# The low part of the shared expert's weights moves from VectorE, in one piece, to GpSimd, in three pieces

## The chip, the cores and the metric

The kernel runs on one core of one Trainium2 chip. The time is that of one execution on the device, in microseconds (us); three runs of the kernel before gave 1497.79, 1499.32 and 1503.46 us, median 1499.32 us. The program is written by hand for the core's engines: TensorE (PE) for matrix products, VectorE (DVE), ScalarE (ACT) and GpSimd (POOL) for elementwise work, SyncE (SP) for starting transfers. Each engine works through its own list in order; the lists meet only at semaphores.

## The reference, cut to what matters

One Perceiver layer over 1024 tokens of width 512: a cross attention, a self attention and a mixture of 16 experts with one shared expert, each behind a layer norm and added to its input.

```python
x = x + xattn(layernorm(x), ctx_512)
x = x + attn(layernorm(x))                 # ends with the product by w_o: 2048 -> 512
x = x + ffn(layernorm(x))

def ffn(x):
    w, sel = route(x)                      # sigmoid scores, best 2 of 4 groups, best 4 of 16 experts
    out = sum over experts e of w[e] * (silu(x @ g[e].T) * (x @ u[e].T)) @ d[e].T
    shared = (silu(x @ shared_gate.T) * (x @ shared_up.T)) @ shared_down.T
    return out + shared
```

## The kernel before, in words

Every matrix product is made of three passes over numbers split in two. A float32 operand a is split into a high part (a cast to the reduced format float32r) and a low part (a minus the high part); hi x hi, hi x lo and lo x hi are summed in PSUM (`mm3`, lines 71 to 73). So each operand costs one cast and one subtraction before TensorE can use it.

The change lies in the last stage, `build_moe`. Its first part handles the 1024 tokens in eight token tiles of 128 (NT = 8, counted from 0). I call it the projection. For token tile tt:

- TensorE makes the product by w_o, 16 blocks of three passes into one PSUM bank. Halfway through (after block 7) it transposes the normalised rows of the tile before, `turn(tt - 1)` (line 1936); after block 11 it makes the router's logits of the tile before; at the end come the sums that give tokens their places (`prefix(tt - 2)`).
- ScalarE casts the attention output to its high part in two halves (`ao_high`, line 1633), copies the high part of the transposed rows (line 1637) and makes the sigmoid (line 1641).
- GpSimd makes the low parts of the two halves (`ao_low`, line 1546, 128x1024 elements each), the reciprocal root of the layer norm (`root`, line 1551), and starts four indirect transfers that scatter rows to their experts' blocks (`scatter`, line 1556).
- VectorE adds the product to the residual (line 1723, named acc below), makes the mean and variance (lines 1726 to 1731), the places of tile tt - 2 (`slots`, lines 1788 to 1791), the normalised rows (`norm`, line 1738, `h_rows` in the trace), then the routing of tile tt - 1 (lines 1749 to 1784, with the low part of the transposed rows, line 1744, between its halves).

I call VectorE's and GpSimd's work for one value of tt a turn. GpSimd's turn is in this order: root(tt), ao_low, two scatters, ao_low, two scatters (the scatters only from tt = 2).

The shared expert's weights (128x3072 elements) are loaded into `raw[0]` (part of the tile `w_ahead`) at the start. In turn 1 ScalarE casts them (line 1659), which raises the semaphore sh_hi; VectorE makes their low part in one subtraction at the end of its turn 1 (line 1866), which raises sh_lo. TensorE waits for sh_lo after the projection, when it begins the shared expert. SP waits for it too, in its loop over tt = 2 to 7, after the load of tile 4: `raw[0]` can then take the weights of routed expert 1 (`w_exp[2]`), which GpSimd needs once the projection is over and all rows are scattered (line 1607).

Two places in the order of work matter. `turn(tt - 1)` needs `norm(tt - 1)`, and the product of tile tt cannot go on past its middle before it. And VectorE's acc of tile tt needs the end of tile tt's product.

Of the kernel before, what the change touches and what calls it, by code (L numbers as in the profile page):

```python
# [25 lines left out]
ALU = mybir.AluOpType  # L26
# [74 lines left out]
def f32(ap):  # L101

    return ap.bitcast(F32)
# [5 lines left out]
def wait(eng, sem, value):  # L109

    if not isinstance(value, int) or value > 0:
        eng.wait_ge(sem, value)
# [1235 lines left out]
NBLK = NE * NT + DUMMY  # L1348
XR, YR, HR = 4, 3, 3
SORT_AT = 8  # L1350
ON_WAY = 3

C_BIAS, C_TRI, C_TRIG, C_DIAG = 0, NE, NE + NE * NE, NE + NE * NE + NG * NG
# [20 lines left out]
def build_moe(nc, ctx, sem, t, keep):  # L1374
# [5 lines left out]
    wcol = gu + NIT * D  # L1380
# [6 lines left out]
    WS = keep["ws"]  # L1387
# [57 lines left out]
    raw = [ahead[:, j * wcol:(j + 1) * wcol] for j in range(2)]  # L1445
    shared = 3 * SLOT
# [25 lines left out]
    sh_hi, sh_lo, e0_hi, e0_lo = sem("sh_hi"), sem("sh_lo"), sem("e0_hi"), sem("e0_lo")  # L1472
# [19 lines left out]
    @block.sync  # L1492
    def _(sp):
        sp.dma_start(acc[:, 0:NT // 2, :], t["x1"][0:NT // 2].rearrange("t p c -> p t c")).then_inc(x1_in[0], 16)
        sp.dma_start(gate_f[:], t["gate_w"]).then_inc(gate_in, 16)
        sp.dma_start(con[:], t["route_c"].to_broadcast([P, C_END])).then_inc(con_in, 16)
        sp.dma_start(tri_p[:], t["tri_p"]).then_inc(con_in, 16)
        sp.dma_start(ones_p[:], t["ones_p"]).then_inc(con_in, 16)
        sp.dma_start(col_p[:], t["col_p"]).then_inc(con_in, 16)
        sp.dma_start(raw[0], t["w_exp"][0]).then_inc(raw_in[0], 16)  # L1500
        sp.dma_start(raw[1], t["w_exp"][1]).then_inc(raw_in[1], 16)
        sp.dma_start(acc[:, NT // 2:, :], t["x1"][NT // 2:].rearrange("t p c -> p t c")).then_inc(x1_in[1], 16)
        for tt in range(2, NT):
            sp.wait_ge(a_lo, 2 * tt - 2)
            sp.dma_start(A[tt % 2], t["ao"][tt]).then_inc(a_in[tt % 2], 16)
            if tt == 4:
                sp.wait_ge(sh_lo, 1)
                sp.dma_start(raw[0], t["w_exp"][2]).then_inc(raw_in[0], 16)
        sp.wait_ge(table_made, 2)
        for j in range(HR):  # L1510
            sp.wait_ge(scattered[j], 16 * TOPK * len(range(j, NT, HR)))

        def block_at(i):
            return sp.value_load(tab[0:1, 2 * NTILE + i:2 * NTILE + i + 1], min_val=0, max_val=NBLK - 1)

        def landed(i):
            sp.wait_ge(y_out[i % YR], 16 * (i // YR + 1))
            sp.sem_inc(y_landed, 1)

        def load_x(i):  # L1520
            wait(sp, x_turned, i - XR + 1)
            sp.dma_start(X[i % XR], t["xs"][bass.ds(block_at(i), 1)].rearrange("o p c -> p (o c)")).then_inc(
                x_in[i % XR], 16)

        for i in range(XR + 2):
            load_x(i)
        for i in range(NTILE):
            if i >= 1:
                landed(i - 1)
            sp.wait_ge(y_made, i + 1)  # L1530
            sp.dma_start(t["xs"][bass.ds(block_at(i), 1)].rearrange("o p c -> p (o c)"), Y[i % YR]).then_inc(
                y_out[i % YR], 16)
            if i + XR + 2 < NTILE:
                load_x(i + XR + 2)
        landed(NTILE - 1)
        for tt in range(NT):
            sp.wait_ge(comb, NT * (TOPK - 1) + tt + 1)
            sp.dma_start(t["out"][tt], acc[:, tt, :]).then_inc(out_sem, 16)
        sp.wait_ge(out_sem, 16 * NT)

    @block.gpsimd
    def _(pool):
        def ao_low(q):
            tt, hf = q // 2, q % 2
            pool.wait_ge(a_hi, q + 1)
            pool.tensor_tensor(AS[q][1], A[tt % 2][:, hf * hh:(hf + 1) * hh, :], f32(AS[q][0]),
                               ALU.subtract).then_inc(a_lo, 1)

        def root(tt):
            pool.wait_ge(ln3, 3 * tt + 3)  # L1550
            pool.tensor_tensor(rstd[tt % 2][:], var[tt % 2][:], eps_pow[:], ALU.pow).then_inc(rstd3, 1)

        def scatter(tt, k):
            if k == 0:
                pool.wait_ge(pos_made, tt + 1)
            pool.indirect_dma_start(rows, bass.IndirectOffsetOnAxis(ap=pos_i[:, tt, k:k + 1], axis=0),  # L1556
                                    HN[:, tt % HR, :], None).then_inc(scattered[tt % HR], 16)

        def slot(e):
            at = e % NSLOT * SLOT  # L1560
            return WS[:, at:at + wcol], WS[:, at + wcol:at + 2 * wcol]

        def expert_low(e):
            pool.tensor_tensor(slot(e)[1], raw[(e + 1) % 2], f32(slot(e)[0]), ALU.subtract).then_inc(w_ready, 1)  # L1564

        def expert_load(e):
            pool.wait_ge(w_ready, e - 1)
            pool.dma_start(raw[(e + 1) % 2], t["w_exp"][e + 1]).then_inc(pool_in[e % 2], 16)

        pool.sem_inc(a_lo, 1)  # L1570
        ao_low(1)
        ao_low(2)
        pool.wait_ge(fill_in, 16 * NBLK // NT)
        for tt in range(NT):
            root(tt)
            if 2 * tt + 3 < 2 * NT:
                ao_low(2 * tt + 3)
            if tt >= 2:
                scatter(tt - 2, 0)
                scatter(tt - 2, 1)  # L1580
            if 2 * tt + 4 < 2 * NT:
                ao_low(2 * tt + 4)
            if tt >= 2:
                scatter(tt - 2, 2)
                scatter(tt - 2, 3)
        for tt in range(NT - 2, NT):
            for k in range(TOPK):
                scatter(tt, k)
        pool.wait_ge(e0_lo, 1)
        pool.sem_inc(w_ready, 1)  # L1590
        expert_load(2)
        for e in range(1, NE):
            if e == NSLOT:
                pool.wait_ge(table_made, 2)
            if e == 1:
                pool.wait_ge(raw_in[0], 32)
            else:
                pool.wait_ge(pool_in[e % 2], 16 * (e // 2))
            if e == 1:
                pool.wait_ge(proj_half, 2 * NT)  # L1600
            elif e < NSLOT:
                pool.wait_ge(d_mm, NT)
            else:
                pool.wait_ge(tile_done, pool.value_load(cum_i[0:1, e - NSLOT:e - NSLOT + 1], min_val=1,
                                                        max_val=NTILE + 1))
            pool.sem_inc(slot_free, 1)
            pool.tensor_copy(slot(e)[0], raw[(e + 1) % 2]).then_inc(pool_hi, 1)  # L1607
            pool.wait_ge(pool_hi, e)
            expert_low(e)
            if e + 2 < NE:  # L1610
                expert_load(e + 2)
        pool.wait_ge(w_ready, NE)
        pool.wait_ge(sorted_made, 1)
        for g in range(NT * TOPK):
            k, tt = g // NT, g % NT
            if tt == 0:
                e = NE - TOPK + k
                pool.wait_ge(y_landed, pool.value_load(cum_i[0:1, e:e + 1], min_val=1, max_val=NTILE + 1))
                pool.sem_inc(gather_free, 1)
            if k < TOPK - 1 and g >= ON_WAY:  # L1620
                pool.wait_ge(g_in[(g - ON_WAY) % 5], 16 * ((g - ON_WAY) // 5 + 1))
            wait(pool, g_in[g % 5], 16 * (g // 5))
            pool.indirect_dma_start(G[g], None, rows,  # L1623
                                    bass.IndirectOffsetOnAxis(ap=pos_si[:, tt, k:k + 1], axis=0)).then_inc(
                                        g_in[g % 5], 16)
# [79 lines left out]
    def _(dve):  # L1705
# [146 lines left out]
        for tt in range(NT):  # L1852
            x2_stats(tt)
            if tt >= 2:
                slots(tt - 2)
            norm(tt)
            if tt == NT - 1:
                break
            if tt >= 1:
                route_groups(tt - 1)  # L1860
            h3_low(tt)
            if tt >= 1:
                route_experts(tt - 1)
            if tt == 1:
                dve.wait_ge(sh_hi, 1)
                dve.tensor_tensor(WS[:, shared + wcol:shared + 2 * wcol], raw[0], f32(WS[:, shared:shared + wcol]),
                                  ALU.subtract).then_inc(sh_lo, 1)
        last = NT - 1
        h3_low(last)
        route_groups(last - 1)  # L1870
# [44 lines left out]
        for i in range(NTILE + 1):  # L1915
# [4 lines left out]
            if i < NTILE:  # L1920
                gated(i)
            if SORT_AT <= i < SORT_AT + 9:
                sort_slots(i - SORT_AT)
            if i >= NTILE - 3:
# [6 lines left out]
    def _(pe):  # L1931
# [61 lines left out]
            if a == 1:  # L1993
                last.then_inc(a_mm, 1)

        pe.wait_ge(sh_lo, 1)
        shared_in(0, 0)
        turn(NT - 1)
        shared_in(0, 1)
# [25 lines left out]
        for tt in range(NT):  # L2025
# [3 lines left out]
            for k in range(NIT):  # L2029
                cols = turned_cols(tt)  # L2030
# [189 lines left out]
```

## Time and profile before

| what | value |
|---|---|
| runs | 1497.79, 1499.32, 1503.46 us |
| time of the profiled execution | 1495.92 us |
| its span in the trace | 1494.1 us |
| busy share of the span: PE, DVE, ACT, POOL | 90%, 54%, 49%, 39% |
| mean granted TensorE clock | 0.958 of full |
| projection (tiles 0 to 7), in the trace | about 1064 to 1178 us |

The span runs from the first to the last recorded instruction; the execution takes 1.8 us more. The busy shares are means over stages with different limits, so the projection is read by itself, from the timeline of each engine: start, duration, instruction, and in square brackets the idle time ahead of it with what ended it. A duration contains the time for which an instruction was held after its start.

### The profile page before, as it was taken

To read this page: it belongs to the slowest core of one execution; us is meant where nothing else is said; L and a number is where in the kernel's file an instruction comes from. 1 tells how busy PE (TensorE), PEld (TensorE's weight loads), DVE (VectorE), ACT (ScalarE), POOL (GpSimd) and SP (SyncE) were. 2 spreads that over 40 slices of the span, in tenths; PEclk is the share of its full clock that TensorE was granted. 3 is DMA by queue.
4 is the path that set the end of the run, shared out by engine and by line. 5 is a ranking of instruction groups with operands and counts; after the bars stand their busy time and mean duration, and the time that the engine had idled before them with its cause. 6 is when DMAs were issued, how large, how long until landed. Compare 5 with 4: busy or idle time off the path is not lost. (4 is left out here: it accounts for less than half of the span.)

```text
span 1494.1 us, 22797 instructions
## 1 busy us (share of the span) xinstructions
PE 1350.1 (90%) x7136; PEld 1107.6 (74%) x7136; DVE 800.1 (54%) x1372; ACT 730.0 (49%) x1736; POOL 585.9 (39%) x350
## 2 busy tenths in 40 slices
PE   5998699999999999999975999998789989999991
PEld 4776577878787878787854888887577867787771
DVE  4434466666666666666634444445278853433235
ACT  2443466565656565656524677777222213343330
POOL 2430233232323333232013333335446486427975
PEclk9998799999999999999987999999799999999996
DMA  5795413141414141412095211112543256536667
GB/s 215 242 285 173 161 66 132 67 159 58 167 53 172 50 175 49 175 49 106 9 323 181 89 64 50 50 50 92 208 149 121 82 184 228 171 124 225 227 210 226
DMA packets 78984, 209.79 MB, mean 140 GB/s; under 512 B 5888, under 2 KB 39168, under 8 KB 72960
## 3 DMA queue, kind: packets, MB, share of 16 engines
q1 hardware_dynamic: 69472, 163.78, 31.4%
q0 software_dynamic: 7136, 38.80, 7.7%
q10 hardware_dynamic: 2304, 6.29, 1.1%
q8 instruction: 40, 0.66, 0.2%
q14 instruction: 32, 0.26, 0.1%
HBM read 154.59 MB, written 92.01 MB: 165 GB/s over the span
## 5 line engine op out<-in xcount | busy, mean ns | idle before, releaser
L722 DVE TENSOR_TENSOR probsT_lo<-psTr,probsT_hi 128x512 fp32r<-128x512 f32 x256 | 176.7, 690 | 168.0 <-ACT probsT_hi L675 167.7
L675 ACT CAST probsT_hi<-psTr 128x512 fp32r<-128x512 f32 x256 | 150.1, 587 | 198.9 <-PE psTr L806 195.1
L806 PE MATMUL psTr<-ident,probs 128*128 128x128 f32 x1024 | 153.6, 274 | 11.3 <-DVE probsT_lo L722 5.2
L806 PEld LDWEIGHTS psTr<-ident,probs 128*128 128x128 f32 x1024 | 124.2, 141 | 50.4 <-DVE probsT_lo L722 13.5
L717 DVE TENSOR_REDUCE nmax<-psS 128x1 f32<-128x1024 f32 x128 | 155.5, 1215 | 9.3 <-PE psS L73 8.3
L588 POOL TENSOR_TENSOR w_slots<-ctx_f,w_slots 128x512 fp32r<-128x512 f32 x32 | 41.4, 1294 | 278.1 <-ACT w_slots L639 278.1
L632 ACT ACTIVATE probs<-psS,nmax 128x1024 f32<-128x1024 f32 x128 | 143.8, 1123 | 12.1 <-DVE nmax L717 12.1
L71 PE MATMUL psS<-w_slots 128*128 128x512 f32 x256 | 113.0, 441 | 3.7 <-DMA w_slots<-qe 2.8
L71 PE MATMUL psV<-probsT_hi,w_slots 128*128 128x512 f32 x256 | 114.7, 448 | 0.6
L71 PE MATMUL bank<-w_slots,ao_first_hi 128*128 (+1 forms) x244 | 102.8, 421 | 8.2 <-POOL w_slots L1564 4.5
L1564 POOL TENSOR_TENSOR w_slots<-w_ahead,w_slots 128x3072 fp32r<-128x3072 f32 x15 | 102.2, 6810 | 1.2
L73 PE MATMUL psS<-w_slots 128*128 128x512 f32 x256 | 101.9, 398 | 0.0
L72 PE MATMUL psS<-w_slots 128*128 128x512 f32 x256 | 101.3, 396 | 0.0
L73 PE MATMUL psV<-probsT_hi,w_slots 128*128 128x512 f32 x256 | 101.1, 395 | 0.0
L72 PE MATMUL psV<-probsT_lo,w_slots 128*128 128x512 f32 x256 | 100.2, 391 | 0.0
L71 PE MATMUL bank<-w_slots 128*128 128x512 f32 (+1 forms) x214 | 87.9, 411 | 8.8 <-DVE w_slots L1904 4.6
L73 PE MATMUL bank<-w_slots,ao_first_lo 128*128 (+1 forms) x244 | 95.8, 393 | 0.0
L72 PE MATMUL bank<-w_slots,ao_first_hi 128*128 (+1 forms) x244 | 95.1, 390 | 0.0
L1274 PEld LDWEIGHTS psSs<-kTs,qT 128*128 128x128 f32 x512 | 77.9, 196 | 9.7
L73 PE MATMUL bank<-w_slots 128*128 128x512 f32 (+1 forms) x214 | 84.9, 397 | 0.0
L72 PE MATMUL bank<-w_slots 128*128 128x512 f32 (+1 forms) x214 | 84.9, 397 | 0.0
L1904 DVE TENSOR_TENSOR w_slots<-bank,w_slots 128x256 fp32r<-128x256 f32 x47 | 19.9, 424 | 117.7 <-ACT w_slots L1686 117.6
(275 smaller groups left out, 3324.8 us busy)
## 6 DMA issues: line engine op xcount, KB each, us to landing
w_ahead<-w_exp POOLq DMA_DIRECT2D x14, 1536.0 KB, 7.8
qe<-stage SPq DMA_DIRECT2D x16, 1024.0 KB, 6.8
w_slots<-qe SPq DMA_DIRECT2D x16, 1024.0 KB, 4.9
wraw<-w_pairs SPq DMA_DIRECT2D x8, 1792.0 KB, 11.2
early<-xs SPq DMA_DIRECT2D x47, 256.0 KB, 3.0
xs<-h_rows SPq DMA_DIRECT2D x47, 256.0 KB, 2.5
early<-ctx SPq DMA_DIRECT2D x16, 512.0 KB, 11.6
ao<-attn_out SPq DMA_DIRECT2D x32, 256.0 KB, 2.4
```

Of the source, the lines that this page charges most:

```text
L71: pe.matmul(out, lhs[0], rhs[0], start=start, stop=False, skip_group_check=True)
L72: pe.matmul(out, lhs[0], rhs[1], start=False, stop=False, skip_group_check=True)
L73: return pe.matmul(out, lhs[1], rhs[0], start=False, stop=stop, skip_group_check=True)
L588: pool.tensor_tensor(CT.lo[:, cols[0], cols[1]], CX[:].rearrange("p (h s) -> p h s", s=S), f32(CT.hi[:, cols[0], cols[1]]), ALU.subtract). ...
L632: act.activation(PR[np_][:, rt, :], psS[rt % 2][:], ACT.Exp, bias=nmax[np_][:, rt:rt + 1], accum_out=rsum[np_][:, rt:rt + 1]).then_inc(exp ...
L675: act.copy(PT[k % PTN].hi[:], psT[slot][:]).then_inc(turned_hi, 1)
L717: dve.tensor_reduce(nmax[np_][:, rt:rt + 1], psS[rt % 2][:], AX.X, ALU.max, negate=True).then_inc(max_made, 1)
L722: dve.tensor_tensor(out, psT[slot][:], f32(hi), ALU.subtract).then_inc(turned_free, 1)
L806: last = pe.transpose(psT[slot][:, q * P:(q + 1) * P], src(q), ident[:])
L1274: last = pe.matmul(psS[j][:, h, :], QB[j][:, h].rearrange("p b s -> p (b s)"), KB[kt][:, g, :], start=False, stop=h == REP - 1, skip_group ...
L1564: pool.tensor_tensor(slot(e)[1], raw[(e + 1) % 2], f32(slot(e)[0]), ALU.subtract).then_inc(w_ready, 1)
L1904: dve.tensor_tensor(HT[i % 2][1], psHT[i % 2][:, 0:I].rearrange("p (k x) -> p k x", k=NIT), f32(HT[i % 2][0]), ALU.subtract).then_inc(ht_l ...
```

## The change

VectorE's subtraction at the end of its turn 1 is taken out. GpSimd makes the same low part in three subtractions of 128x1024 elements, one at the end of its turns 1, 2 and 3 (behind the scatters, where there are any). Each waits for sh_hi and raises sh_lo by one, so TensorE and SP wait for 3 instead of 1. SP's wait, with the load of `w_exp[2]` behind it, moves from behind the load of tile 4 to behind that of tile 6.

```diff
+SHARED_AT = (1, 2, 3)
...
-            if tt == 4:
-                sp.wait_ge(sh_lo, 1)
+            if tt == 6:
+                sp.wait_ge(sh_lo, len(SHARED_AT))
                 sp.dma_start(raw[0], t["w_exp"][2]).then_inc(raw_in[0], 16)
...
+        def shared_low(part):
+            n = wcol // len(SHARED_AT)
+            cols = slice(part * n, (part + 1) * n)
+            pool.wait_ge(sh_hi, 1)
+            pool.tensor_tensor(WS[:, shared + wcol:shared + 2 * wcol][:, cols], raw[0][:, cols],
+                               f32(WS[:, shared:shared + wcol][:, cols]), ALU.subtract).then_inc(sh_lo, 1)
...
             if tt >= 2:
                 scatter(tt - 2, 2)
                 scatter(tt - 2, 3)
+            if tt in SHARED_AT:
+                shared_low(SHARED_AT.index(tt))
...
-            if tt == 1:
-                dve.wait_ge(sh_hi, 1)
-                dve.tensor_tensor(WS[:, shared + wcol:shared + 2 * wcol], raw[0], f32(WS[:, shared:shared + wcol]),
-                                  ALU.subtract).then_inc(sh_lo, 1)
...
-        pe.wait_ge(sh_lo, 1)
+        pe.wait_ge(sh_lo, len(SHARED_AT))
```

VectorE's list from the end of its turn 1 to the start of turn 2, before (`choice_x` to `choice_weight` are the routing of tile 0, `acc` is the residual sum of tile 2):

```order
L1779 TENSOR_TENSOR choice_x<-choice,scores 128x64
L1780 TENSOR_REDUCE choice_w<-choice_x 128x4
L1781 TENSOR_REDUCE choice_sum<-choice_w 128x1
L1782 TENSOR_SCALAR choice_sum<-choice_sum 128x1
L1783 RECIPROCAL choice_sum<-choice_sum 128x1
L1784 TENSOR_SCALAR choice_weight<-choice_w,choice_sum 128x4
L1866 TENSOR_TENSOR w_slots<-w_ahead,w_slots 128x3072
L1723 TENSOR_TENSOR acc<-bank,acc 128x512
```

and the same place in the changed kernel, whose lines are numbered ten higher:

```order
L1792 TENSOR_SCALAR choice_sum<-choice_sum 128x1
L1793 RECIPROCAL choice_sum<-choice_sum 128x1
L1794 TENSOR_SCALAR choice_weight<-choice_w,choice_sum 128x4
L1733 TENSOR_TENSOR acc<-bank,acc 128x512
L1736 BN_STATS st_0<-acc 128x6
```

The residual sum of tile 2 now stands directly behind the routing of tile 0.

GpSimd's list from the end of its turn 1 to the start of its turn 4, in the changed kernel (L1568 is a piece, `rstd` is root, L1547 is ao_low, L1557 the scatters, two to a row):

```order
L1547 TENSOR_TENSOR ao_first_lo<-early,ao_first_hi 128x1024
L1568 TENSOR_TENSOR w_slots<-w_ahead,w_slots 128x1024
L1552 TENSOR_TENSOR rstd_0<-var_0,eps_pow 128x1
L1547 TENSOR_TENSOR w_slots<-early,w_slots 128x1024
L1557 DMA xs<-h_rows,slot_int 18432x512 x2
L1547 TENSOR_TENSOR ao_first_lo<-early,ao_first_hi 128x1024
L1557 DMA xs<-h_rows,slot_int 18432x512 x2
L1568 TENSOR_TENSOR w_slots<-w_ahead,w_slots 128x1024
L1552 TENSOR_TENSOR rstd_1<-var_1,eps_pow 128x1
L1547 TENSOR_TENSOR w_slots<-early,w_slots 128x1024
```

Before, root of the next tile stands where the pieces stand; the first piece comes directly behind an ao_low, the second (and the third, a turn later) behind two scatters.

## Rows read from the trace of the kernel before

**Rows 1.** The page: span and instructions.
```profile
span 1494.1 us, 22797 instructions
```
**Rows 2.** Timeline, TensorE: turn of tiles 2 and 4 (tile tt's transposes).
```profile
1112.17 1.11 PE L1936 MATMUL bank<-ident,h_rows 128*128 128x128 f32 x4 [3.83 <-DVE h_rows L1738]
1142.17 0.66 PE L1936 MATMUL bank<-ident,h_rows 128*128 128x128 f32 x4 [0.64 <-DVE h_rows L1738]
```
**Rows 3.** Busy time by stretch: PE, PEld, DVE, ACT, POOL, clock, DMA share, GB/s.
```profile
1102.50:1113.00 10.50, 6.67 (x32) 5.38 (x31) 9.75 (x18) 1.05 (x1) 3.88 (x3) 0.92 0.45 158
1113.00:1118.00 5.00, 5.00 (x14) 3.94 (x13) 4.79 (x10) 1.53 (x2) 4.11 (x4) 0.50 0.82 268
```
**Rows 4.** Timeline, ScalarE: casts released by the ends of tiles 2, 3, 4.
```profile
1102.53 1.05 ACT L1633 CAST w_slots<-early 128x1024 fp32r<-128x1024 f32 x1 [2.72 <-PE bank L73]
...
1122.51 1.05 ACT L1633 CAST w_slots<-early 128x1024 fp32r<-128x1024 f32 x1 [2.72 <-PE bank L73]
...
1135.73 1.05 ACT L1633 CAST w_slots<-early 128x1024 fp32r<-128x1024 f32 x1 [2.72 <-PE bank L73]
```
**Rows 5.** Timeline, VectorE: ends of turns 1 to 3, starts of turns 2 to 5.
```profile
1103.11 0.23 DVE L1784 TENSOR_SCALAR choice_weight<-choice_w,choice_sum 128x4 f32<-128x4 f32 x1
1103.37 3.36 DVE L1866 TENSOR_TENSOR w_slots<-w_ahead,w_slots 128x3072 fp32r<-128x3072 f32 x1
1106.65 0.68 DVE L1723 TENSOR_TENSOR acc<-bank,acc 128x512 f32<-128x512 f32 x1
...
1120.54 0.23 DVE L1784 TENSOR_SCALAR choice_weight<-choice_w,choice_sum 128x4 f32<-128x4 f32 x1
1122.51 0.69 DVE L1723 TENSOR_TENSOR acc<-bank,acc 128x512 f32<-128x512 f32 x1 [1.74 <-PE bank L73]
...
1136.29 0.23 DVE L1784 TENSOR_SCALAR choice_weight<-choice_w,choice_sum 128x4 f32<-128x4 f32 x1
1136.56 0.69 DVE L1723 TENSOR_TENSOR acc<-bank,acc 128x512 f32<-128x512 f32 x1
...
1150.60 0.69 DVE L1723 TENSOR_TENSOR acc<-bank,acc 128x512 f32<-128x512 f32 x1
```
**Rows 6.** Timeline, GpSimd: last instructions of turns 1 to 3, root(4), first expert cast.
```profile
1097.26 2.37 POOL L1546 TENSOR_TENSOR ao_first_lo<-early,ao_first_hi 128x1024 fp32r<-128x1024 f32 x1 [2.64 <-ACT ao_first_hi L1633]
...
1118.84 0.96 POOL L1556 DMA_INDIRECT xs<-h_rows,slot_int  x1 [0.31 <-issue]
...
1134.26 0.96 POOL L1556 DMA_INDIRECT xs<-h_rows,slot_int  x1 [0.31 <-issue]
1138.71 0.57 POOL L1551 TENSOR_TENSOR rstd<-var,eps_pow 128x1 f32<-128x1 f32 x1 [3.48 <-DVE var L1731]
...
1211.12 2.78 POOL L1607 CAST w_slots<-w_ahead 128x3072 fp32r<-128x3072 f32 x1
```
**Rows 7.** Three lines of VectorE: duration ns min/median/max, first and last start.
```profile
L1769 DVE TENSOR_TENSOR cmp_experts<-masked x8: 412/1368/2374, 1097.5 to 1191.9; 128x256 f32<-128x256 f32 x8
L1770 DVE TENSOR_TENSOR cmp_experts<-masked x8: 410/416/2593, 1099.8 to 1192.2; 128x256 f32<-128x256 f32 x8
L1791 DVE CAST slot_int<-slot_all x8: 170/2368/2417, 1109.3 to 1198.5; 128x4 int32<-128x4 f32 x8
```
**Rows 8.** Timeline near 645 us: GpSimd, and VectorE beside it.
```profile
644.99 2.14 POOL L127 TENSOR_TENSOR kv_rope_second<-early 128x1024 f32<-128x1024 f32 x1
...
645.88 0.17 DVE L772 RECIPROCAL rinv<-rsum 128x4 f32<-128x4 f32 x1
```
**Rows 9.** TensorE after two idle times elsewhere, and the stretch after the first.
```profile
141.03 0.46 PE L71 MATMUL psE<-w_slots 64*128 64x512 f32 x1 [2.24 <-DVE stage L348]
1302.93 0.49 PE L71 MATMUL bank<-w_slots 128*128 x1 [2.15 <-DVE w_slots L1904]
142.00:146.00 4.00, 4.00 (x9) 2.19 (x8) 1.97 (x3) 1.76 (x3) 0.00 (x0) 0.50 0.12 33
```
**Rows 10.** The page's list of transfers: an expert's weights, us to landing.
```profile
w_ahead<-w_exp POOLq DMA_DIRECT2D x14, 1536.0 KB, 7.8
```

## The prediction

> **What bounds the kernel now.** I read the page first: the span is 1494.1 us [rows 1], and the profiled execution took 1495.92 us, 1.8 more. That is 3.40 us under the median of the runs, 1499.32. I sum against the profiled execution and add these 3.40 us at the end. Then I went to the chain of waits of the projection, which passes through VectorE's acc and norm and comes back to TensorE at its transposes. So I read the timelines of TensorE, VectorE and GpSimd side by side.
>
> Two things are to be seen. First, TensorE stands still for 3.83 us in the middle of tile 3, at the transposes of tile 2, because `h_rows` is late [rows 2]. Its granted clock is 0.92 over the stretch with the stop and 0.50 in the 5 us behind it, the lower of its two levels, 1.2 GHz [rows 3]. ScalarE's casts show what this costs: tile 3 takes 1122.51 - 1102.53 = 19.98 us, tile 4 takes 1135.73 - 1122.51 = 13.22 us [rows 4]. The difference is 6.76 us: 3.83 of standing still and 2.93 of slow clock.
>
> The cause is the instruction that the change removes: VectorE's L1866 starts at 1103.37 and the next acc only at 1106.65 [rows 5], while tile 2's product was ready at 1102.53.
>
> Second, VectorE is the bound by itself in the turns behind. From acc at 1136.56 to acc at 1150.60 it takes 14.04 us [rows 5] against TensorE's 13.22, and TensorE waits 0.64 us at the transposes of tile 4 [rows 2]. It does so again, with the same time, for tiles 5 and 6. So what VectorE loses in turn 3 is not made up before the projection's end, and what it wins counts only as far as it wins it. Tile 7 and all that follows hang on this chain and move as one.
>
> VectorE is slow there because it is held. L1770 normally takes 416 ns and once 2593, L1769 412 and up to 2374, the cast L1791 170 and up to 2417 [rows 7]; each long one begins while GpSimd is in an ao_low of 2.37 us [rows 6] and ends with it. Not every instruction is held: a reciprocal, with one SBUF input, took 0.17 us at 645.88, in the middle of GpSimd's 2.14 us [rows 8]. Held are those with two SBUF inputs (L1769, L1770), a cast and the `h_rows` TENSOR_SCALAR from SBUF to SBUF.
>
> **Part 1: the subtraction leaves VectorE, piece 1 comes to turn 1.** Removed: 1106.65 - 1103.37 = 3.28 us between the routing and acc [rows 5]. Piece 1 has the shape of an ao_low, 128x1024, so 2.37 us [rows 6]. ScalarE's cast has raised sh_hi long before, so it begins at once behind the ao_low that ends at 1097.26 + 2.37 = 1099.63, and lasts to 1102.0. VectorE is then in the middle of L1769 to L1771, all with two SBUF inputs. One of them is held: 2593 - 416 = 2177 ns, 2.18 us [rows 7]. Bounds: 1.96 by L1769, 2.25 by L1791 [rows 7], and nothing if VectorE gets in first each time. I take 2.18 because L1770's row is the one where it lost against GpSimd with its neighbour just finished. Acc of tile 2 comes 3.28 - 2.18 = 1.10 us earlier.
>
> The stop at the transposes of tile 2 shrinks to 3.83 - 1.10 = 2.73 us. If the clock falls again, tile 3 ends at 1122.51 - 1.10 = 1121.41. If it holds, the product would be 2.93 us earlier still, but then VectorE is the later one (part 2).
>
> **Part 2: piece 2 in turn 2.** GpSimd's last scatter ends at 1118.84 + 0.96 = 1119.80 [rows 6], now 1118.70, so the piece ends at 1121.07, or up to 0.3 later, the gap that GpSimd leaves ahead of a scatter [rows 6]. L1784 would start at 1120.54 - 1.10 = 1119.44 [rows 5] and, as a TENSOR_SCALAR from SBUF to SBUF, is held until then. Acc of tile 3 can start at 1121.1 to 1121.4. Tile 3's product ends at 1121.41. Cost 0: VectorE's old wait of 1.74 us for TensorE [rows 5] is the cover. It is used up, though, so a clock that holds brings at most some 0.3 us.
>
> **Part 3: piece 3 in turn 3.** The last scatter ends at 1134.26 + 0.96 = 1135.22 [rows 6], the piece at 1137.59 in the old times. L1784 stood at 1136.29 and acc at 1136.56 [rows 5]; now acc cannot start before 1137.6 to 1137.9. That costs 1.05 to 1.35 us, and here there is no cover: VectorE was 0.83 us behind TensorE already (1136.56 against 1135.73, [rows 4, 5]). I take 1.2. Below: 0, if a TENSOR_SCALAR of four elements is not held. Above: 1.8, if L1782, 0.4 us ahead of it, is held too.
>
> The Trainium skill (SBUF — State Buffer, "Who interferes with whom") says that the port pair shared by VectorE and GpSimd is an exclusive lock, so whoever starts first blocks the other for the whole instruction, and that a VectorE instruction with two SBUF inputs is hit by a GpSimd one that reads SBUF. The long L1769 and L1770 agree. By this rule moving work to GpSimd pays only where VectorE has no such instruction meanwhile, and each of the three pieces falls on one.
>
> The same skill (VectorE: DVE Perf Modes, "Mode 2×_2P") gives tensor_scalar between SBUF tiles the mode that takes both ports when the outermost dimension above one is even, which holds for the four columns of L1784 and not for the one of L1782. By it part 3 costs about 1.2; without it, 0. No row shows L1784 beside a long GpSimd instruction.
>
> **What else moves.** GpSimd's roots stand behind the pieces. The tightest is root(4), which begins at 1138.71 after 3.48 us of idle time [rows 6]; piece 3 is done 0.8 to 1.1 us earlier, and root(4) itself moves back with VectorE. Nothing waits. SP's load of expert 1's weights goes from 1107 to about 1138 us; it lands in about 7.8 us [rows 10] and is used at 1211.12 [rows 6]. Behind it on SP stands only the load of tile 7, released at about 1142. TensorE's wait for sh_lo comes 40 us after piece 3. All these cost 0; the cover of the load is some 65 us.
>
> **The sum.** -3.28 + 2.18 + 0 + 1.2 = +0.1 us. The profiled execution would take 1496.0 us, the median 1499.32 + 0.1 = 1499.4. The gain of turn 2 is handed back in turn 3.
>
> **Rivals.**
>
> (a) The clock falls in tile 5 (slower). With part 3 the stop at the transposes of tile 4 grows from 0.64 to 1.84 us [rows 2]. For it: after an idle time of 2.24 us the granted clock was 0.50 soon behind [rows 9]. Against: after 2.15 us matmuls went on at full pace [rows 9]. [...] Price: 2.93 less the 0.83 us by which VectorE is behind, 2.1. Time 1499.4 + 2.1 = 1501.5; with part 3 at 1.8, 1502.1.
>
> (b) L1784 isn't held, so pieces 2 and 3 cost nothing. Then -1.10 stands: 1498.2. If the clock also holds after 2.73 us, acc of tile 3 follows VectorE: 1120.77 - 1.10 = 1119.67, which is 2.84 earlier than 1122.51: 1496.5. For it: pieces 2 and 3 lie mostly beside short one-input instructions. Against: L1791, also four columns, is held [rows 7].
>
> (c) The pieces hold VectorE nowhere, the full gain. Acc of tile 2 at 1103.37, one turn of 14.04 later acc of tile 3 at 1117.41 instead of 1122.51: -5.1, 1494.2. Even here VectorE's pitch eats part of the 6.76. Against it stand the long rows [rows 7].
>
> (d) The change doesn't do what it says, because GpSimd's pieces come late and push its root, and with it norm: only if a piece took over 3.3 us. No row of that shape does.
>
> **Chances.** Forecast 0.60 (own range 1498.9 to 1500.3), (a) 0.14, (b) 0.16, (c) 0.08, (d) 0.02. A difference of 0.5%, 7.5 us, is about what a measurement of this kernel can tell from no change, and no case reaches it: the largest, (c), is 0.34%. What is left is scatter of the runs, whose three times lie within 5.7 us. So faster 0.04, same 0.92, slower 0.04. The range goes from just inside (c) to just above (a): 1495.2 to 1502.6.
>
> **What would show it.** Right: no L1866; three GpSimd subtractions of 2.4 us ending near 1102, 1121 and 1137.7; a long duration of L1769, L1770 or L1771 near 1102 and of L1784 (four columns) in turns 2 and 3; acc of tile 2 at about 1105.5; the stop at the transposes of tile 2 at 2.7 us, and of tile 4 at 1.8. Wrong: L1784 at 0.23 us beside a piece (b), acc of tile 2 at 1103.4 (c), or a granted clock of 0.5 in tile 5 (a).

## The result, and the profile after

The changed kernel is slower: median 1504.47 us (22 runs, 1501.36 to 1507.68) against 1500.80 us (22 runs, 1497.79 to 1507.90) for the kernel before, run beside it. The ratio is 1.0022, 95% interval 1.0013 to 1.0032, that is 3.3 us slower (2.0 to 4.8). The forecast was +0.1 us.

The page of the changed kernel gives the span of its profiled execution:

```profile
span 1501.8 us, 22798 instructions
```

That is 7.7 us over the span of before [rows 1], more than the runs differ. The acc of VectorE divides it: 1.67 us lie ahead of acc of tile 1 (1091.23 against 1089.56), where the programs are alike; 3.86 between acc of tile 1 and of tile 7; 2.17 behind. The change acts in the middle stretch, and 3.86 us agrees with the 3.3 of the runs. Of the 2.17 behind, 1.25 lie between acc of tile 7 and the next sum into acc, behind the projection, where TensorE stands still for 2.51 us in both kernels and its clock falls behind that stop in the changed kernel alone (the last section comes back to this). Executions of one kernel differ by several us elsewhere, so from here on I read distances within the projection and not spans.

VectorE's timeline in the changed kernel, the acc of tiles 1 to 7 (start, duration, instruction, idle time ahead with its cause). It answers to [rows 5]:

```profile
1091.23 0.69 DVE L1733 TENSOR_TENSOR acc<-bank,acc 128x512 f32<-128x512 f32 x1 [5.53 <-PE bank L73]
...
1107.24 0.69 DVE L1733 TENSOR_TENSOR acc<-bank,acc 128x512 f32<-128x512 f32 x1
...
1124.14 0.69 DVE L1733 TENSOR_TENSOR acc<-bank,acc 128x512 f32<-128x512 f32 x1
...
1141.37 0.69 DVE L1733 TENSOR_TENSOR acc<-bank,acc 128x512 f32<-128x512 f32 x1
...
1156.11 0.69 DVE L1733 TENSOR_TENSOR acc<-bank,acc 128x512 f32<-128x512 f32 x1 [0.50 <-PE bank L73]
...
1170.16 0.69 DVE L1733 TENSOR_TENSOR acc<-bank,acc 128x512 f32<-128x512 f32 x1
...
1183.38 0.69 DVE L1733 TENSOR_TENSOR acc<-bank,acc 128x512 f32<-128x512 f32 x1 [1.11 <-PE bank L73]
```

From one acc to the next I call the length of a turn. Before: 17.09, 15.86, 14.05, 14.04, 14.04, 13.21 for turns 1 to 6, 88.29 in all. After: 16.01, 16.90, 17.23, 14.74, 14.05, 13.22, 92.15 in all. Turn 1 won 1.08 us, turn 2 lost 1.04, turn 3 lost 3.18, turn 4 lost 0.70.

VectorE's timeline shows why: here are the instructions that were held, and `choice_weight` beside them, which was not (its line is 1794 here, 1784 before; L1784 here is the selection `sel`):

```profile
1099.20 2.37 DVE L1779 TENSOR_TENSOR cmp_experts<-masked 128x256 f32<-128x256 f32 x1
...
1101.50 2.62 DVE L1780 TENSOR_TENSOR cmp_experts<-masked 128x256 f32<-128x256 f32 x1
...
1119.41 3.00 DVE L1784 TENSOR_SCALAR sel<-rank 128x16 f32<-128x16 f32 x1
...
1123.88 0.23 DVE L1794 TENSOR_SCALAR choice_weight<-choice_w,choice_sum 128x4 f32<-128x4 f32 x1
...
1136.84 3.14 DVE L1787 TENSOR_TENSOR choice<-rank,route_rows 128x64 f32<-128x64 f32 x1
```

and GpSimd's timeline round the pieces (L1568), which answers to [rows 6]:

```profile
1098.92 2.37 POOL L1547 TENSOR_TENSOR ao_first_lo<-early,ao_first_hi 128x1024 fp32r<-128x1024 f32 x1 [2.64 <-ACT ao_first_hi L1643]
1101.25 2.59 POOL L1568 TENSOR_TENSOR w_slots<-w_ahead,w_slots 128x1024 fp32r<-128x1024 f32 x1
...
1119.02 0.96 POOL L1557 DMA_INDIRECT xs<-h_rows,slot_int  x1 [0.30 <-issue]
1120.01 2.36 POOL L1568 TENSOR_TENSOR w_slots<-w_ahead,w_slots 128x1024 fp32r<-128x1024 f32 x1
...
1136.48 0.96 POOL L1557 DMA_INDIRECT xs<-h_rows,slot_int  x1 [0.31 <-issue]
1137.47 2.42 POOL L1568 TENSOR_TENSOR w_slots<-w_ahead,w_slots 128x1024 fp32r<-128x1024 f32 x1
```

Three things are to be seen. In turn 1, ao_low and piece 1 stand back to back, and each holds one instruction, L1779 and then L1780, until its own end. In turns 2 and 3 the held instruction is not `choice_weight`, as forecast, but `sel` and `choice`, eight and six instructions ahead of it. And it starts 0.60 and 0.63 us before the piece's recorded start, while the last scatter still runs, yet ends with the piece (1122.41 against 1122.37; 1139.98 against 1139.89).

TensorE's timeline shows who waits for that (L1958 is the sum over the selection for the token places, L1942 the transposes; to be read beside [rows 2]), and lines of busy time by stretch show the clock behind the last two stops (PE, PEld, DVE, ACT, POOL, granted clock, DMA share, GB/s; beside [rows 3]):

```profile
1105.77 0.40 PE L1958 MATMUL bank<-sel,tri_tokens 128*128 128x16 f32 x2 [1.66 <-DVE sel_before L1786]
...
1112.83 0.66 PE L1942 MATMUL bank<-ident,h_rows 128*128 128x128 f32 x4 [0.86 <-DVE h_rows L1748]
...
1122.67 0.40 PE L1958 MATMUL bank<-sel,tri_tokens 128*128 128x16 f32 x2 [2.34 <-DVE sel_before L1786]
...
1146.93 1.11 PE L1942 MATMUL bank<-ident,h_rows 128*128 128x128 f32 x4 [3.25 <-DVE h_rows L1748]
```

```profile
1123.00:1126.00 3.00, 3.00 (x10) 2.43 (x10) 2.48 (x9) 0.00 (x0) 0.00 (x0) 0.51 0.00 0
1146.00:1153.00 7.00, 6.07 (x28) 5.24 (x28) 6.63 (x16) 1.53 (x2) 5.58 (x5) 0.76 0.70 224
```

The stop of 3.83 us in tile 3 is gone, divided into 1.66 at the end of tile 2 and 0.86 at the transposes, without a fall of the clock. In its place stand 2.34 us at the end of tile 3 and 3.25 us at the transposes of tile 4. The clock falls behind both: the mean granted clock is 0.51 from 1123 to 1126 us, practically the lower level, and 0.76 over the seven us round the second stop, because the first matmuls run at the lower level.

### The profile page after: what moved, and what is told of

Same layout as the page of the kernel before. It is cut to its first block and busy times, and to the rows that moved or that the text cites. A ratio compares the mean times of both kernels' runs of the same rounds, so it can differ in the third digit from the quotient of the medians.

```text
span 1501.8 us, 22798 instructions
## 1 busy us (share of the span) xinstructions
PE 1357.7 (90%) x7136; PEld 1111.9 (74%) x7136; DVE 805.6 (54%) x1371; ACT 730.3 (49%) x1736; POOL 593.7 (40%) x353
## 5 line engine op out<-in xcount | busy, mean ns | idle before, releaser
L632 ACT ACTIVATE probs<-psS,nmax 128x1024 f32<-128x1024 f32 x128 | 143.7, 1123 | 12.2 <-DVE nmax L717 12.2
L71 PE MATMUL bank<-w_slots 128*128 128x512 f32 (+1 forms) x214 | 89.1, 416 | 8.5 <-DVE w_slots L1910 4.4
L73 PE MATMUL bank<-w_slots 128*128 128x512 f32 (+1 forms) x214 | 86.0, 402 | 0.0
L72 PE MATMUL bank<-w_slots 128*128 128x512 f32 (+1 forms) x214 | 85.9, 401 | 0.0
```

What stands on the lines that cost most here:

```text
L71: pe.matmul(out, lhs[0], rhs[0], start=start, stop=False, skip_group_check=True)
L72: pe.matmul(out, lhs[0], rhs[1], start=False, stop=False, skip_group_check=True)
L73: return pe.matmul(out, lhs[1], rhs[0], start=False, stop=stop, skip_group_check=True)
L632: act.activation(PR[np_][:, rt, :], psS[rt % 2][:], ACT.Exp, bias=nmax[np_][:, rt:rt + 1], accum_out=rsum[np_][:, rt:rt + 1]).then_inc(exp ...
```

## The experiments

The table gives the length of VectorE's turns in each kernel's profiled execution, in us; kernels 2, 3, 7 and 8 were run once, for this profile. The lengths repeat within 0.05 us where nothing acts on them, so differences of a few tenths can be read from one profile.

| kernel | turn 1 | 2 | 3 | 4 | 5 | 6 | sum | ratio of times to before (95%) |
|---|---|---|---|---|---|---|---|---|
| before | 17.09 | 15.86 | 14.05 | 14.04 | 14.04 | 13.21 | 88.29 | |
| changed | 16.01 | 16.90 | 17.23 | 14.74 | 14.05 | 13.22 | 92.15 | 1.0022 (1.0013 to 1.0032) |
| 1: low part left out | 14.04 | 14.05 | 14.04 | 14.03 | 14.04 | 13.21 | 83.41 | 0.9991 (0.9963 to 1.0019) |
| 2: piece 3 only | 13.82 | 14.07 | 16.86 | 14.02 | 14.05 | 13.18 | 86.00 | |
| 3: piece 2 only | 13.82 | 16.88 | 14.02 | 14.03 | 14.03 | 13.22 | 86.00 | |
| 4: pieces ahead of scatters | 16.02 | 16.25 | 16.24 | 14.40 | 14.04 | 13.22 | 90.17 | 1.0014 (0.9990 to 1.0038) |
| 5: pieces beside acc | 14.01 | 14.29 | 14.23 | 14.02 | 14.05 | 13.21 | 83.81 | 0.9972 (0.9958 to 0.9986) |
| 6: on VectorE in turn 0 | 14.07 | 14.06 | 14.04 | 14.05 | 14.04 | 13.21 | 83.47 | 0.9970 (0.9954 to 0.9987) |
| 7: before, load moved | 17.09 | 15.91 | 14.05 | 14.04 | 14.03 | 13.22 | 88.34 | |
| 8: pieces behind the selection | 16.03 | 16.82 | 16.56 | 14.01 | 14.03 | 13.22 | 90.67 | |

**Experiment 1: what the removed instruction is worth.** Edit, on the kernel before; the low part of the shared expert's weights is left out by it:

```diff
-                dve.tensor_tensor(WS[:, shared + wcol:shared + 2 * wcol], raw[0], ...).then_inc(sh_lo, 1)
+                dve.sem_inc(sh_lo, 1)
```

> The kernel before with VectorE's subtraction left out and nothing in its place (the low part of the shared expert's weights isn't made; the rest is unchanged). What the removed instruction is worth by itself. Theory A (VectorE's pitch is the bound behind it): acc of tile 2 comes 3.3 us earlier, turn 2 takes VectorE's own 14.0 us, acc(1) to acc(7) is 88.3 - 5.1 = 83.2 us, ratio to before 0.9966. Rival (TensorE's stop and slow clock were the whole cost): 6.8 us less, 81.5 us, ratio 0.9955.

Measured: 83.41 us from acc of tile 1 to that of tile 7, 4.88 less than before, where theory A said 5.1 and the rival 6.8. VectorE's timeline, acc of tiles 1 to 3 and 7:

```profile
1088.90 0.69 DVE L1723 TENSOR_TENSOR acc<-bank,acc 128x512 f32<-128x512 f32 x1 [5.54 <-PE bank L73]
...
1102.94 0.69 DVE L1723 TENSOR_TENSOR acc<-bank,acc 128x512 f32<-128x512 f32 x1 [0.26 <-DVE choice_weight L1784]
...
1116.99 0.69 DVE L1723 TENSOR_TENSOR acc<-bank,acc 128x512 f32<-128x512 f32 x1
...
1172.31 0.69 DVE L1723 TENSOR_TENSOR acc<-bank,acc 128x512 f32<-128x512 f32 x1 [1.11 <-PE bank L73]
```

Acc of tile 3 doesn't wait for TensorE: VectorE's own 14.04 us is the length of each turn. The 0.26 us ahead of acc of tile 2 go with the semaphore that VectorE still raises there; without it turn 1 is 13.82 (experiments 2 and 3). So taking the whole instruction off VectorE is worth 4.9 us here, 5.1 without the semaphore, and not TensorE's stop and slow clock of 6.76. The interval of the timed runs, 0.9963 to 1.0019, leaves out the rival's 0.9955 and has theory A's 0.9966 at its edge, but it can't tell this kernel from the one before.

**Experiments 2 and 3: one piece at a time.** Edit, on the changed kernel (with the waits for sh_lo set to 1): piece 3 only, and likewise piece 2 only (`part != 1`); the other two thirds of the low part are left out:

```diff
         def shared_low(part):
+            if part != 2:
+                return
```

> The changed kernel with only the piece of turn 3 made (the other two thirds of the low part are left out). Theory H (each GpSimd piece holds VectorE): turn 2 takes 14.0 us instead of 16.9, turn 3 stays at 17.2 (a hold of about 2.9 us), tile 5 still has its stop and slow clock, so turn 4 is 14.7. Rival L (turns 2 and 3 are long because of the moved load or of work that GpSimd has piled up): turn 3 falls back to about 14.0 as well.

> The changed kernel with only the piece of turn 2 made (the other two thirds are left out). Theory H: acc(1) to acc(2) is 13.8 us, turn 2 is 14.0 + 2.9 = 16.9, turns 3 and 4 are 14.0 each, no slow clock in tile 5. Rival L: turn 2 at 14.0 or turn 3 still long.

Measured: the piece alone makes its turn long, 16.86 in turn 3 and 16.88 in turn 2, and no other turn. In both kernels SP's load stands at its new place, so rival L falls. VectorE's timeline in the kernel with piece 3 only, and then in the one with piece 2 only:

```profile
1134.37 3.01 DVE L1786 TENSOR_SCALAR sel<-rank 128x16 f32<-128x16 f32 x1
```

```profile
1117.94 3.00 DVE L1786 TENSOR_SCALAR sel<-rank 128x16 f32<-128x16 f32 x1
```

The selection is held for 3.0 us in either; 3.01 - 0.17 = 2.84 is what the turn gained over 14.04 (2.82). Expectations of experiment 2 that missed: turn 3 is 16.86 us and not 17.2, and turn 4 is 14.02 and not 14.7, because the slow clock in tile 5 did not come with piece 3 alone. TensorE's timeline there:

```profile
1137.64 0.40 PE L1960 MATMUL bank<-sel,tri_tokens 128*128 128x16 f32 x2 [2.27 <-DVE sel_before L1788]
...
1144.73 0.66 PE L1944 MATMUL bank<-ident,h_rows 128*128 128x128 f32 x4 [0.91 <-DVE h_rows L1750]
```

The hold is paid at the end of tile 4's product (2.27 us), which leaves 0.91 for the transposes. In turn 3 of the changed kernel it was `choice` that was held, behind the selection. TensorE got past the tile's end and the whole delay came at the transposes, 3.25 us. So which of two neighbours is held decides where TensorE stands still.

It does not decide by itself whether the clock falls. In turn 2 the changed kernel and experiment 3 hold the same instruction and stop TensorE at the same place, for 2.34 and 2.33 us. In the changed kernel the clock then falls to 0.51 (the line from 1123 to 1126 above); in experiment 3 it stays at full:

```profile
1121.50:1124.50 3.00, 3.00 (x16) 2.52 (x16) 2.48 (x9) 0.00 (x0) 0.00 (x0) 1.00 0.00 0
```

No run here shows why. What it costs is shown: with the clock at full, turn 3 of experiment 3 takes 14.02 us.

**Experiment 4: pieces ahead of the last two scatters.** Edit, on the changed kernel:

```diff
+            if tt in SHARED_AT:
+                shared_low(SHARED_AT.index(tt))
             if tt >= 2:
                 scatter(tt - 2, 2)
                 scatter(tt - 2, 3)
-            if tt in SHARED_AT:
-                shared_low(SHARED_AT.index(tt))
```

> The changed kernel with the pieces of turns 2 and 3 ahead of the last two scatters instead of behind them, so directly behind an ao_low. Theory S (a piece queued behind a scatter takes hold of VectorE about 0.6 us before its recorded start, so that place costs 2.9 and not 2.2): turn 2 is 14.0 + 2.2 = 16.2 us instead of 16.9, turn 3 16.2 instead of 17.2, acc(1) to acc(7) 1.7 to 2.4 us shorter than the changed kernel's 92.1, ratio to before 1.001. Rival (a piece costs the same wherever it stands): within 0.3 us of 92.1, ratio 1.0025.

Measured: turns 2 and 3 are 16.25 and 16.24 us, as theory S said (16.2), and the sum is 1.98 shorter than the changed kernel's. Turn 2 on VectorE and then on GpSimd:

```profile
1117.31 2.44 DVE L1779 TENSOR_TENSOR cmp_experts<-masked 128x256 f32<-128x256 f32 x1
1119.68 2.61 DVE L1780 TENSOR_TENSOR cmp_experts<-masked 128x256 f32<-128x256 f32 x1
```

```profile
1117.08 2.38 POOL L1547 TENSOR_TENSOR ao_first_lo<-early,ao_first_hi 128x1024 fp32r<-128x1024 f32 x1
1119.40 2.61 POOL L1568 TENSOR_TENSOR w_slots<-w_ahead,w_slots 128x1024 fp32r<-128x1024 f32 x1
```

The same work costs 2.20 us here (16.25 - 14.05) and 2.8 behind a scatter. It still costs almost the whole piece. The timed ratio, 0.9990 to 1.0038, can't tell this kernel from the changed one, nor from the one before.

**Experiment 5: pieces beside VectorE's unshared work.** Edit, on the changed kernel:

```diff
             pool.wait_ge(sh_hi, 1)
+            pool.wait_ge(routed, part + 1)
...
                 route_experts(tt - 1)
+            if tt in SHARED_AT:
+                dve.sem_inc(routed, 1)
```

> The changed kernel in which each piece also waits for the end of VectorE's routing of its turn (a semaphore that VectorE raises just ahead of acc), so that it runs beside acc, the statistics and the variance, which have at most one SBUF input and no two-port form. Theory H: those aren't held; the piece of 2.4 us outlasts them by about 0.3 to 0.4 and delays root by as much. acc(1) to acc(2) 13.8 us, turns 2 to 4 about 14.4 each, acc(1) to acc(7) 84.0 to 84.8 us (before 88.3, changed 92.1), ratio to before 0.997. No long duration in the routing beyond that of ao_low. Rival (GpSimd holds VectorE's statistics and residual sum too): each turn 16 us or more, 90 us, ratio 1.001.

Measured: 83.81 us, ratio 0.9972 (0.9958 to 0.9986), faster than both kernels. VectorE from acc of tile 3 on, then GpSimd:

```profile
1119.96 0.69 DVE L1734 TENSOR_TENSOR acc<-bank,acc 128x512 f32<-128x512 f32 x1 [0.23 <-DVE choice_weight L1795]
1120.81 0.69 DVE L1737 BATCH_NORM_STATS2 st<-acc 128x6 f32<-128x512 f32 x1 [0.16 <-DVE acc L1734]
...
1122.14 0.28 DVE L1800 TENSOR_TENSOR choice_x<-choice,slot_of 128x64 f32<-128x64 f32 x1
...
1122.91 2.61 DVE L1749 TENSOR_SCALAR h_rows<-acc,mv,rstd 128x512 f32<-128x512 f32 x1
```

```profile
1119.94 2.40 POOL L1569 TENSOR_TENSOR w_slots<-w_ahead,w_slots 128x1024 fp32r<-128x1024 f32 x1 [1.51 <-DVEq L1876]
1122.30 0.57 POOL L1552 TENSOR_TENSOR rstd<-var,eps_pow 128x1 f32<-128x1 f32 x1
```

Beside the piece (1119.94 to 1122.34) acc and the statistics take their 0.69 us. Only L1800, with two SBUF inputs, is touched, for 0.05 us at the piece's end. Root follows the piece at once, about 0.2 us later than the variance would allow, but that costs nothing: turn 4 has a late root too and takes 14.02. What turns 1 to 3 lose (14.01 against 13.82, 14.29 and 14.23 against 14.05) is the semaphore that VectorE raises ahead of acc, about 0.2 us each; turn 4 has none. The rival falls. The same three subtractions on the same engine cost 8.3 us less, 83.81 against 92.15, for one semaphore.

**Experiment 6: the work stays on VectorE, in turn 0.** Edit, on the kernel before:

```diff
-            if tt == 1:
+            if tt == 0:
                 act.wait_ge(raw_in[0], 16)
...
-            if tt == 1:
+            if tt == 0:
                 dve.wait_ge(sh_hi, 1)
```

> The kernel before (VectorE makes the low part in one piece) with ScalarE's cast and VectorE's subtraction moved from turn 1 to turn 0, where VectorE waits 5.5 us for TensorE. Theory P (VectorE's pitch is what counts, and only from turn 1 on): acc(0) to acc(1) longer by 0 to 0.5 us because ao_low and the subtraction hold each other, acc(1) to acc(2) 13.8 to 14.1, then 14.0 each: acc(0) to acc(7) 96.4 to 97.0 us against 101.3 before and 105.2 changed, ratio to before 0.9968. Rival (the subtraction, held by or holding ao_low, only shifts TensorE's stop to tile 2): acc(0) to acc(7) stays within 1 us of 101.3.

Measured: acc of tile 0 to acc of tile 7 is 96.47 us (13.00 + 83.47), within the expected 96.4 to 97.0; ratio 0.9970 (0.9954 to 0.9987). VectorE, then GpSimd:

```profile
1093.59 3.35 DVE L1866 TENSOR_TENSOR w_slots<-w_ahead,w_slots 128x3072 fp32r<-128x3072 f32 x1
...
1099.20 0.69 DVE L1723 TENSOR_TENSOR acc<-bank,acc 128x512 f32<-128x512 f32 x1 [2.27 <-PE bank L73]
```

```profile
1093.97 5.21 POOL L1546 TENSOR_TENSOR ao_first_lo<-early,ao_first_hi 128x1024 fp32r<-128x1024 f32 x1 [2.65 <-ACT ao_first_hi L1633]
```

The hold works the other way round too: VectorE's subtraction began first and ran its normal 3.35 us, and ao_low, begun 0.38 later, took 5.21 us instead of 2.38. TensorE waited 0.17 us for it. VectorE still waits 2.27 us for TensorE ahead of acc of tile 1, so the subtraction is free.

**Experiment 7: the moved load alone.** Edit, on the kernel before: `if tt == 4:` to `if tt == 6:` in SP's loop.

> The kernel before with only SP's load of expert 1's weights moved from behind the load of tile 4 to behind that of tile 6. All theories of mine: no cost, acc(1) to acc(7) 88.3 us, and the first cast of expert weights on GpSimd follows the last scatter as before. Rival L (the moved load delays something): any pitch of turns 4 to 7 over 14.1 us or GpSimd waiting for the weights.

Measured: 88.34 us against 88.29, and GpSimd's first cast of expert weights begins at 1212.93, behind the last scatter (1211.38 + 0.96) and the start of a transfer, with no wait for the weights. No cost, rival L falls a second time.

**Experiment 8: pieces behind the selection.** Edit, on the changed kernel:

```diff
             pool.wait_ge(sh_hi, 1)
+            pool.wait_ge(sel_made, SHARED_AT[part])
```

> The changed kernel in which each piece also waits for VectorE's selection of its turn (the sum sel_before, which raises a semaphore just ahead of choice). In the changed kernel the selection itself was held from 0.6 us before the piece's recorded start. Theory W (GpSimd reaches for the shared port as soon as the piece's semaphores are up, even while the scatter ahead of it is still recorded): the selection passes at 0.17 us, one of the two or three instructions with two SBUF inputs right behind it is held until the piece ends, turns 1 to 3 lose 2.2 to 2.6 us each, 16.3 to 16.6 us in turns 2 and 3, TensorE doesn't wait for the selection at the ends of tiles 2 to 4 any more, acc(1) to acc(7) about 90 to 91 us. Rival D (the scatter's descriptor writing itself holds VectorE there): the selection or the add is still held while the scatter runs, turns 2 and 3 stay at 16.9 and 17.2 us.

Measured: turns 2 and 3 on VectorE, then on GpSimd:

```profile
1119.53 0.17 DVE L1785 TENSOR_SCALAR sel<-rank 128x16 f32<-128x16 f32 x1
...
1119.84 0.22 DVE L1788 TENSOR_TENSOR choice<-rank,route_rows 128x64 f32<-128x64 f32 x1
1120.09 2.88 DVE L1790 TENSOR_TENSOR choice_x<-choice,scores 128x64 f32<-128x64 f32 x1
...
1136.73 0.22 DVE L1788 TENSOR_TENSOR choice<-rank,route_rows 128x64 f32<-128x64 f32 x1
1136.99 2.54 DVE L1790 TENSOR_TENSOR choice_x<-choice,scores 128x64 f32<-128x64 f32 x1
```

```profile
1119.48 0.96 POOL L1557 DMA_INDIRECT xs<-h_rows,slot_int  x1 [0.30 <-issue]
1120.47 2.40 POOL L1569 TENSOR_TENSOR w_slots<-w_ahead,w_slots 128x1024 fp32r<-128x1024 f32 x1
...
1136.06 0.96 POOL L1557 DMA_INDIRECT xs<-h_rows,slot_int  x1 [0.30 <-issue]
1137.05 2.39 POOL L1569 TENSOR_TENSOR w_slots<-w_ahead,w_slots 128x1024 fp32r<-128x1024 f32 x1
```

In turn 2 the selection passes at 0.17 us, 0.05 us after the scatter's start; `choice` passes 0.36 us into it; L1790, the next instruction with two SBUF inputs, starts 0.38 us before the piece's recorded start and is held to its end. Turn 2 would prove little by itself, since the piece starts 13.19 us behind acc of tile 2 here and not 12.77, so that the selection is clear of it anyway. Turn 3 is the cleaner case: `choice` passes 0.67 us into the scatter and 0.32 us ahead of the piece's recorded start, where the changed kernel's `choice` was held 0.63 us ahead. So the scatter alone does not hold VectorE, and rival D falls. In the kernel before too `sel` and `choice` pass beside the same scatter, at 1118.89 and 1119.19:

```profile
1118.84 0.96 POOL L1556 DMA_INDIRECT xs<-h_rows,slot_int  x1 [0.31 <-issue]
1118.89 0.17 DVE L1774 TENSOR_SCALAR sel<-rank 128x16 f32<-128x16 f32 x1
1119.10 0.18 DVE L1776 TENSOR_TENSOR sel_before<-sel_before,sel 128x16 f32<-128x16 f32 x1
1119.19 0.22 DVE L1777 TENSOR_TENSOR choice<-rank,route_rows 128x64 f32<-128x64 f32 x1
```

Theory W's place for the hold came out. Its size did for turn 3 (16.56) and not for turn 2, 16.82 instead of 16.3 to 16.6. The shape fits a piece that reaches for the port as soon as its semaphores are up, but these runs show it only by when the holds begin; GpSimd's record doesn't show what it does between.

## Why the prediction was wrong

**Part 1 held.** Acc of tile 2 was forecast 1.10 us earlier and came 1.08 earlier. The hold on L1780 was forecast at 2.18 and is 2.62 - 0.42 = 2.20. The full price of the removed instruction in rival (c), 5.1 us, is 4.88 in experiment 1.

**Part 2 is the step that failed.** It said that `choice_weight` "is held until then", at a cost of 0, since VectorE's wait of 1.74 us covers it. Held was the selection, which stands 1.65 us earlier in the turn (1118.89 against 1120.54 before) and has 1.7 us of short instructions behind it. A hold ends when the piece ends, and all that stands behind the held instruction comes after that. I had reckoned with a start 13.15 us behind acc of tile 2, which let `sel` pass 0.9 us ahead of the piece and `choice` 0.6. It began at 12.77, because the transposes ran at full clock and ao_low no longer waited for ScalarE, and the hold had set in 0.60 us ahead of that (experiment 8 puts this apart from the scatter): 1.0 us too early for my margin. The piece took 2.83 us from VectorE (3.00 - 0.17), not the 1.4 to 1.7 that I had set against the cover (1121.1 to 1121.4 against 1119.67). Turn 2 became 16.90 and not 15.86. The forecast for the end of piece 2 itself was good: 15.13 us after acc of tile 2, forecast 15.5.

**Part 3 failed by the same step.** Forecast 1.2, "above: 1.8", measured 3.18. Of it 2.92 is the hold on `choice` (3.14 - 0.22); experiment 2 gives 2.8 for piece 3 alone. The other 0.26 is what turn 2 left behind: the clock fell behind the wait of 2.34 us, the transposes of tile 3 came late, and ao_low behind them held L1780 until later than it had held L1769 before. The wait alone does not do that: experiment 3 has it too, at full clock, and loses nothing in turn 3. My upper bound took the wrong instruction, so the true value lay outside it.

**A waiter was left out.** I followed acc and norm, but TensorE also waits for the selection at the end of each product. It showed no wait before only because the selection was early.

**Rival (a) came true on top, for less.** The stop at the transposes of tile 4 was 3.25 us and not 1.84, and the clock fell. Turn 4 lost 0.70 and not 2.1, because the clock was back at full in the fifth us behind the stop, where it had taken until the seventh before, and VectorE's own lag covered most. I had tied rival (a) to tile 5 alone; the clock fell in tile 4 as well. In tile 3, where parts 1 and 2 reckoned with a fall, it stayed at full.

**The rest.** GpSimd's roots, the moved load and the late sh_lo cost nothing (experiment 7, and turns 5 and 6 at their old lengths). The sum is -1.08 + 1.04 + 3.18 + 0.70 + 0.02 = +3.86, against a forecast of -1.1 + 0 + 1.2 = +0.1. The rules of the Trainium skill that I cited did hold: the port pair is an exclusive lock (SBUF — State Buffer, "Who interferes with whom"). The changed kernel shows VectorE held by a piece (3.00 us for 0.17), experiment 6 GpSimd held by VectorE (5.21 for 2.38). Which VectorE instruction a piece meets is not in the rule, and it decided the size; nor is it that the hold can begin 0.6 us ahead of the piece's recorded start. The rule on the mode of tensor_scalar (VectorE: DVE Perf Modes, "Mode 2×_2P") agrees too, by `sel`, a TENSOR_SCALAR of sixteen columns that was held for 3.00 us; the four columns of `choice_weight` never met a piece.

## What to carry to other kernels

Work moved from VectorE to GpSimd is not hidden by GpSimd being idle: its price is the time for which it holds a VectorE instruction with two SBUF inputs, or a cast or TENSOR_SCALAR between SBUF tiles, and that time can exceed the work's own length (2.92 us for a piece of 2.42). Put it where VectorE reads PSUM or one SBUF input, and say so with a semaphore (experiment 5, 8.3 us better than without), or leave it on VectorE in a turn in which VectorE waits anyway (experiment 6). When a hold is reckoned, take the earliest instruction that it could catch, count all that queues behind it, and list every engine that waits for any of them.

## What the runs showed of the hardware that I had not expected

- A GpSimd subtraction queued directly behind an indirect transfer's start held VectorE before its own recorded start: 0.60 to 0.63 us before in the changed kernel and experiments 2 and 3, 0.38 in turn 2 of experiment 8. In turn 3 of the changed kernel `sel_before`, 0.73 us ahead, still passed. Directly behind another subtraction there is no such lead: the hold of the second began when one VectorE instruction had slipped in between (1101.50, 0.25 us after the record).
- Of two GpSimd subtractions back to back each lets one waiting VectorE instruction through at its end, and the next is caught: L1779 and L1780 in one turn. GpSimd's second one is then recorded at 2.58 to 2.61 us instead of 2.38.
- The length of TensorE's stop did not decide whether its granted clock fell. It fell to 0.5 behind stops of 3.83 us (before), 3.25 and 2.34 (changed), and 2.76 and 1.88 (experiment 8, tiles 3 and 4). It stayed at full behind 2.27 (experiment 2), 2.33 (experiment 3) and 1.66 (changed). The same stop of 2.5 us behind the projection (at L1958 in the kernel before) was followed within 3 us by 0.5 in the changed kernel and experiments 1, 2, 3, 5, 6 and 8, and by a full clock in the kernel before and experiments 4 and 7. In these three the way from acc of tile 7 to the next sum into acc was 31.8 to 31.9 us, in the others 33.0 or more. One profile of each does not tie this to the edits; it shows how times of one kernel can differ by a us or more.
